# A graph network with a 64-expert layer: the experts' down products as three split matmuls

## What is computed

```python
hg = jnp.einsum('ecd,efd->ecf', expert_in, w_gate)      # 64 experts, up to 117 tokens each, 512 -> 256
hu = jnp.einsum('ecd,efd->ecf', expert_in, w_up)
expert_out = jnp.einsum('ecf,edf->ecd', jax.nn.silu(hg) * hu, w_down)   # 256 -> 512
```

## Time and profile before

| | us |
|---|---|
| median of three runs | 1040.75 (1038.95 to 1041.92) |
| the profiled execution, its own time | 1040.16 |
| its span | 1038.3 |
| product of the first expert to that of expert 62 (line 1375) | 684.05 to 1000.16 |
| one expert in that stretch | 5.10 |

### The profile page before, as it was taken

How to read it: one execution, slowest core, us unless ns; L and a number is a source line. 1 busy time by engine, 2 the same in 40 slices (tenths; PEclk the granted TensorE clock), 3 DMA queues, 4 the chain that set the end, 5 groups by cost and what they waited for, 6 DMA issues and landing times. The chain is left out here.

```text
span 1038.3 us, 13178 instructions
## 1 busy us (share of the span) xinstructions
PE 940.6 (91%) x4324; PEld 696.8 (67%) x4324; DVE 709.4 (68%) x1325; ACT 447.8 (43%) x694; POOL 392.2 (38%) x322
## 2 busy tenths in 40 slices
PE   2979598996999999998999989889999999999980
PEld 2879585443888778886788868666666666666650
DVE  4463548988665467678767786758777776766675
ACT  3442510013344353543444522466666666666640
POOL 4500000000750035410751115366666666666640
PEclk9985898998999999999999998989999999999995
DMA  6200003312420022201220052559999999999868
GB/s 173 83 1 1 1 1 118 121 57 88 133 72 23 1 80 92 83 1 51 87 86 17 20 186 87 187 196 328 338 339 334 355 333 324 380 348 345 312 161 209
DMA packets 57100, 159.73 MB, mean 154 GB/s; under 512 B 13840, under 2 KB 21590, under 8 KB 48595
## 3 DMA queue, kind: packets, MB, share of 16 engines
q1 hardware_dynamic: 44755, 147.63, 41.7%
q0 software_dynamic: 12288, 11.36, 3.8%
HBM read 152.71 MB, written 25.58 MB: 172 GB/s over the span
## 5 line engine op out<-in xcount | busy, mean ns | idle before, releaser
L260 PE MATMUL ps<-split_operands 128*125 128x512 f32 (+5 forms) x690 | 272.9, 396 | 31.4 <-DVE split_operands L986 5.7
L261 PE MATMUL ps<-split_operands 128*125 128x512 f32 (+5 forms) x690 | 266.1, 386 | 0.0
L262 PE MATMUL ps<-split_operands 128*125 128x512 f32 (+5 forms) x690 | 265.4, 385 | 0.0
L630 POOL DMA_INDIRECT yrow_scratch<-work,row_i x64 | 150.9, 2358 | 97.3 <-ACT work L891 94.8
L260 PEld LDWEIGHTS ps<-split_operands 128*125 128x125 f32 (+3 forms) x690 | 135.0, 196 | 61.3 <-issue 13.6
L376 POOL TENSOR_TENSOR split_operands<-work,split_operands 128x512 fp32r<-128x512 f32 x66 | 83.6, 1296 | 202.1 <-ACT split_operands L358 189.9
L262 PEld LDWEIGHTS ps<-split_operands 128*125 128x125 f32 (+3 forms) x690 | 135.2, 196 | 26.7
L261 PEld LDWEIGHTS ps<-split_operands 128*125 128x125 f32 (+3 forms) x690 | 135.6, 196 | 24.0
L1366 DVE TENSOR_TENSOR gate_up_lo<-expert_weights,split_operands 128x2048 fp32r<-128x2048 f32 x64 | 146.3, 2286 | 3.8 <-ACT split_operands L873 3.6
L873 ACT ACTIVATE split_operands<-expert_weights 128x2048 fp32r<-128x2048 f32 x64 | 121.9, 1905 | 3.2 <-DMA expert_weights<-experts_in 3.1
L1834 PE MATMUL ps<-expert_weights,work 128*117 128x512 f32 x256 | 120.3, 592 | 0.5 <-issue 0.5
(11 more groups left out here) (214 smaller groups left out, 1286.3 us busy)
## 6 DMA issues: line engine op xcount, KB each, us to landing
expert_weights<-experts_in SPq DMA_DIRECT2D x64, 1024.0 KB
expert_weights<-experts_in SPq DMA_DIRECT2D x64, 512.0 KB
work<-w_in SPq DMA_DIRECT2D x12, 1024.0 KB, 5.2
yrow_scratch<-work SPq DMA_DIRECT2D x5, 1500.0 KB
split_operands<-yrow_scratch SPq DMA_DIRECT2D x4, 1120.0 KB
work<-wmix_in SPq DMA_DIRECT2D x4, 1024.0 KB, 7.6
work<-cw_in SPq DMA_DIRECT2D x3, 1024.0 KB, 5.2
work<-rows_in SPq DMA_DIRECT2D x10, 256.0 KB, 4.7
```

What stands on the lines that cost most here:

```text
L260: pe.matmul(o, a[1], b[0], start=start, stop=False)
L261: pe.matmul(o, a[0], b[1], start=False, stop=False)
L262: return pe.matmul(o, a[0], b[0], start=False, stop=stop)
L630: pool.indirect_dma_start(yrow, bass.IndirectOffsetOnAxis(ap=row_i[:, e:e + 1], axis=0), OS[e % 4], None, bounds_check=last_row, oob_is_er ...
```

## The change

The down product of each expert is made as `gate_up` is, with `mm3`: both operands get a high and a low part.

- The down weights get a high part in one of two places (`DN_hi`), made by ACT in a new step `down_hi(e)`, and a low part in place in the ring (`DN_lo`), made by DVE in `down_lo(e)`.
- The copy at the end of `gated(e)` (line 1379) is gone. ACT makes the high part of the transposed hidden values out of PSUM (`h_part_hi(e)`), and DVE the low part (`h_part_lo(e)`), into a new tile `HTP`.
- `down(e)` issues six split matmuls in place of two fp32 ones and waits for `down_lo(e)` as well. `halves_done` counts the parts in their new order.
- Streams: ACT now runs `silu(e)`, `gate_up_hi(e+2)`, `scale(e-1)`, `h_part_hi(e)`, `down_hi(e+1)`, `xe_hi(e+2)`; DVE runs `gated(e)`, `gate_up_lo(e+2)`, `h_part_lo(e)`, `down_lo(e+1)`, `xe_lo(e+2)`, and `gates` where there is one.

```diff
+        DN_hi = [rg(o, 1024) for o in (16272, 32144)]
+        DN_lo = [sb(f"down_lo{r}", [P, 1024], F32R, at=rg_at + 4 * (o + WA)) for r, o in enumerate(ring_at)]
...
+        HTP = sb("hidden_pairs", [P, 8 * CAP], F32R, at=fg_at + 4 * 4416)
+        HTR = [(HTP[:, cut(4 * CAP * i, 2 * CAP)], HTP[:, cut(4 * CAP * i + 2 * CAP, 2 * CAP)]) for i in range(2)]
...
+        def halves_done(e, down):
+
+            if down:
+                return len(plan) + min(2 * e + 3, 2 * E)
+            return len(plan) + max(2 * e, 1)
...
+            def down_hi(e):
+                act.wait_ge(S(f"load_in{RINGS + e % RINGS}"), 16 * (e // RINGS) + 16)
+                if e >= 2:
+                    act.wait_ge(S("o_ps"), e - 1)
+                act.activation(DN_hi[e % 2], RING[e % RINGS][:, cut(WA, 1024)], ACT.Copy).then_inc(S("weight_hi"), 1)
+
+            def h_part_hi(e):
+                act.wait_ge(S("ht_ps"), NSH + e + 1)
+                if e >= 2:
+                    act.wait_ge(S("o_ps"), e - 1)
+                act.activation(HTR[e % 2][0][:, 0:2 * CAP], ps[:, 4 + e % 2, 0:2 * CAP], ACT.Copy).then_inc(S("ht_hi"), 1)
...
+            down_hi(0)
             for e in range(E):
                 silu(e)
                 if e + 2 < E:
                     gate_up_hi(e + 2)
                 if e >= 1:
                     scale(e - 1)
+                h_part_hi(e)
+                if e + 1 < E:
+                    down_hi(e + 1)
                 if e + 2 < E:
                     xe_hi(e + 2)
...
-                dve.wait_ge(S("weight_hi"), len(plan) + e + 1)
+                dve.wait_ge(S("weight_hi"), halves_done(e, False))
...
-                dve.wait_ge(S("ht_ps"), NSH + e + 1)
+
+            def down_lo(e):
+                dve.wait_ge(S("weight_hi"), halves_done(e, True))
+                dve.tensor_tensor(DN_lo[e % RINGS][:], RING[e % RINGS][:, cut(WA, 1024)], f(DN_hi[e % 2]), ALU.subtract).then_inc(S("weight_lo"), 1)
+
+            def h_part_lo(e):
+                dve.wait_ge(S("ht_hi"), NT * NL + e + 1)
                 if e >= 2:
                     dve.wait_ge(S("o_ps"), e - 1)
-                dve.tensor_copy(HTF[e % 2], ps[:, 4 + e % 2, 0:2 * CAP]).then_inc(S("ht_sb"), 1)
+                dve.tensor_tensor(HTR[e % 2][1][:, 0:2 * CAP], ps[:, 4 + e % 2, 0:2 * CAP], f(HTR[e % 2][0][:, 0:2 * CAP]),
+                                  ALU.subtract).then_inc(S("ht_sb"), 1)
...
+            down_lo(0)
             for e in range(E):
                 gated(e)
                 if e + 2 < E:
                     gate_up_lo(e + 2)
+                h_part_lo(e)
+                if e + 1 < E:
+                    down_lo(e + 1)
+                if e + 2 < E:
                     xe_lo(e + 2)
...
-                pe.wait_ge(S("weight_lo"), len(plan) + e + 1)
+                pe.wait_ge(S("weight_lo"), halves_done(e, False))
...
+                pe.wait_ge(S("weight_lo"), halves_done(e, True))
                 for k in range(2):
-                    last = pe.matmul(ps[0:CAP, 6 + e % 2, :], HTF[e % 2][:, cut(k * CAP, CAP)], RING[e % RINGS][:, cut(WA + 512 * k, 512)],
-                                     start=(k == 0), stop=(k == 1))
+                    last = mm3(ps[0:CAP, 6 + e % 2, :], sub(HTR[e % 2], A_, cut(k * CAP, CAP)),
+                               (DN_hi[e % 2][:, cut(512 * k, 512)], DN_lo[e % RINGS][:, cut(512 * k, 512)]), k == 0, k == 1)
```

## The result

The changed kernel takes 1057.13 us (median of four runs, 1054.55 to 1058.99), the kernel before beside it 1041.34 (1038.95 to 1043.64): a ratio of 1.0165, 95% interval 1.0128 to 1.0201. It is slower, by 1.3 to 2.0%. The forecast was 1056.5 us, slower with a chance of 0.91.

A forecast was written before the change was run, and what follows sets the result against it. PE was taken to bound the kernel before, a two-expert latency chain the changed one. 1040.16 + 11.5 (chain) + 4.4 (router's steps) = 1056.1, other terms 0; with the median above the profiled run, forecast 1056.5 us, range 1047 to 1069.

The forecast's parts named there:

- The main step: Loop from product(e-1) through PE, ACT and DVE to product(e+1) becomes the bound: 10.57 us for two experts, +11.5 us.
- One reading: In the kernel before, DVE's largest stall, after the product, waits until ACT has the high part of the next weights.
- PE's work: Six split matmuls of `down` take 1.40 us in place of 1.71: 0.31 less per expert, to 4.80.
- The router's steps: DVE steps between `xe_lo` and the next product, e = 2 to 9, now count in full: about +4.4 us.
- The clock: PE's clock stays at 1.00 through the stage.
- Transfers: Loads spread over 5.28 us per expert in place of 5.10, late ones rarer: taken as 0, up to +3 us allowed.
- POOL: `down_lo` may hold up scatters, with room for it; a scatter under way does not hold up `down_lo`: 0.
- rival 2: The same chain with a POOL scatter holding up `down_lo`: 18 us more, 1075; chance 0.07.
- Start and end: `down_hi(0)` and `down_lo(0)` fall into stalls before the first product; the last chain gains +0.4 - 0.3; both taken as 0.
- The first rival: PE stays the bound, 1021 us, or the transfers take over, 1030 to 1040; chance 0.06.

The follow-up runs named there:

- The filler in two places: ACT copy of 128 x 234 added to the changed kernel between `silu` and `gate_up_hi` (1064.7 us) or behind `down_hi` (1053.98); first place in kernel before: 1039.7.
- the transposes inside: Changed kernel with PE issuing the two transposes of product(e-1) after the first of four blocks of `gate_up(e)`, not ahead of it: 1039.9 us.
- a quarter of `down_lo`: Changed kernel with `down_lo` cut to 256 of 1024 columns, one matmul reading the high part instead of the low: 1037.89 us.
- both moves: Changed kernel with the transposes inside and the router's DVE steps moved to right behind the product: 1039.66 us, again 1036.68.
- the three orders: The last experiment: both moves, plus `transpose_x(e+2)` ahead of `down(e-1)` on PE and `xe_lo(e+2)` ahead of `down_lo(e+1)` on DVE: 1036.0 us.
- `down` inside too: Both moves, plus `down(e-2)` issued after the first block of `gate_up(e)`, ahead of the transposes: 1096.92 us.

## Why the prediction was right

**The main step held: a latency chain of two experts takes PE's place.** Forecast 10.57 us, measured 10.53, by steps 4.12 / 4.10, 0.28 / 0.28, 1.95 / 1.94, 2.20 / 2.21, 0.33 / 0.31, 1.14 / 1.13, 0.55 / 0.56. The mean of products 10 to 60 is 5.26 in place of 5.28, and it was 5.09: 5.264 - 5.092 over 62 experts is 10.7 us, forecast 11.5. The filler in two places and the transposes inside show that it is this chain. PE's period is 0.46 above its work of 4.80, as forecast (0.5), though only 0.33 of it counts as idle, since the modelled ends of its matmuls reach into the gaps; DVE is idle for 0.64 (forecast 0.75).

One reading was off and carried nothing. In the kernel before, DVE's largest stall is not the one for ACT's high part (3.6 us in all, seven times) but the one for PE's transposes, ahead of the copy: 61.8 us, before each of the 62. The two end almost together, though. In the earlier trace rows the high part is done at 869.27 and the copy starts at 869.00, so the copy did stand beside the wait for ACT, and its successor does not.

**PE's work.** Six matmuls follow each other by 0.23 us (868.30, 868.53 and so on to 869.46), so 1.40 in all as forecast, 0.31 less than before. It gave nothing, since PE waited; only in the last experiment does it show in full, for some twenty experts.

**The router's steps.** The first ten experts took 59.97 us for 51.32, 8.7 more. Of these 1.7 are the chain's and about 1.5 a drop of the clock, which leaves 5.4, forecast 4.4. The steps themselves take what they took:

```profile
705.20 0.48 DVE L1418 TENSOR_TENSOR work<-work 125x320 f32<-125x320 f32 x1
706.65 0.42 DVE L1401 TENSOR_TENSOR work<-ps,work 117x256 f32<-117x256 f32 x1
707.13 0.42 PE L1882 MATMUL ps<-ident,work 117*128 117x117 f32 x2 [1.83 <-DVE work L1401]
```

**The clock** was forecast to stay at 1.00, and did but for one place. PE had been idle for the 1.83 us above (in the window below it was busy for 3.17 of 5 us), and then:

```profile
700.00:705.00 5.00, 4.83 (x25) 3.53 (x23) 4.01 (x4) 4.54 (x7) 2.95 (x2) 1.00 0.82 252
705.00:710.00 5.00, 3.17 (x15) 2.31 (x14) 4.86 (x9) 2.99 (x5) 3.84 (x3) 0.83 0.95 300
710.00:715.00 5.00, 5.00 (x23) 3.94 (x22) 2.55 (x5) 2.67 (x4) 0.24 (x1) 0.82 0.78 263
```

The granted clock (third column from the right) fell from its 2.4 GHz to 1.2 GHz for some 3.5 us. From first matmul to `down` that `gate_up` took 4.41 us (707.72 to 712.13) in place of 2.88, so 1.5 us. The gap does not settle it, though. Both fillers in the changed kernel left PE idle for the same 1.83 and 1.82 us before the same transposes, and there the clock stayed at 1.00 and the product came 1.1 us sooner after the one before (5.05 for 6.15). So a drop here is one of two outcomes, and these runs do not show what decides.

**Transfers.** No `gate_up_hi` waited for a load; six had. The share of the stretch fell from 0.94 to 0.89. As forecast.

**POOL.** 62 `down_lo` took 1215 ns in the mean, no more than the one of the earlier trace rows, and nearly all began inside a scatter, so no scatter under way held them up: rival 2 is out. The other direction did show, and a little more than before: 59 scatters that started inside `gate_up_lo` took 2.41 us, and the gather, 1.08 before, took 1.19 when it started inside `down_lo`. POOL had room for it. The page "SBUF — State Buffer" of the Trainium skill (section "SBUF: two separate sides") says that whichever of the two starts first keeps the other out for its whole instruction, for a DVE instruction with two SBUF inputs only against a GpSimd one that reads SBUF. These traces agree only where DVE was first.

**Start and end, both put at 0, were off and cancel.** Product 0 came 4.58 us later, of which 4.1 were there before the experts began (the last product of the shared experts at 668.72 for 664.59); the clock was lower in this execution, 0.58 for 0.74 from 620 to 640 us. That is chance and not the change: over the twelve traces product 0 goes with the clock there (see the experiments), and with as much of the low clock as the kernel before had, changed kernels have it at 683.58 and 682.87, not later than its 684.05. The last product came 6.87 us after that of expert 62 for 6.31. And from the last product to the end of the span it was 28.0 us for 31.8. DVE waited less for the gathered rows of the first choices to be added after it, 0.35 us in the changed kernel

```profile
1034.58 3.40 DVE L1436 SCALAR_TENSOR_TENSOR x_out<-split_operands,work,x_out 125x512 f32<-125x512 f32 x5 [0.35 <-DMA split_operands<-yrow_scratch]
```

and 4.85 in the one before:

```profile
1016.03 3.40 DVE L1403 SCALAR_TENSOR_TENSOR x_out<-split_operands,work,x_out 125x512 f32<-125x512 f32 x5 [4.85 <-DMA split_operands<-yrow_scratch]
```

This repeats: with the filler in the changed kernel 27.2 and 27.8 us, in the kernel before 32.3, with a quarter of `down_lo` 31.5. So the slower loop gives 3 to 4 us back at its end. But the pace alone does not sort the runs: the router's steps moved early (5.27 per expert) had 29.2, the transposes inside (5.01) 29.1, both moves 29.8 and 29.5, the three orders (4.97) 28.9. I think that the rows' transfers find the loads done earlier; that is argued and was not tried, and the cause stays open. The sum is 4.58 + 17.57 + 0.56 - 3.81 = 18.9 us of span, where 15.9 were forecast. That the median came out within 0.6 us of the forecast is luck: several terms were off by 1 to 5 us and made up for each other. The stretch, +17.6 for +15.9, is the fair test.

**What I had not read**: the second chain at 5.0, just below; that DVE is full, at 5.58, in the experts with router steps; and how soon the loads come late below 5.0. None changes this forecast, but together they leave nothing to win: even with the orders put right, this change gives nothing. The first rival, faster by up to 19 us, was capped by the loads at 1030 to 1040, and the last experiment, with its other orders, landed there, at 1036.0.

## What to carry to other kernels

An engine that is 70% busy has no room to give if its idle time lies in front of one particular instruction: ask on which side of that stall the new work is placed, and add up the loop from this instruction through the other engines' streams back to it, over as many iterations as there are buffers. Work put behind the stall (here 1.47 us on DVE in each turn of two experts, for 0.31 us of PE saved in each expert) lengthens the loop; the same filler costs 7 to 8 us on the loop and nothing off it. Write down every such loop, not only the longest: a second at 5.0 us stood right under the first, and one move made a third of 6.06. And look at the next bound before spending effort on the first: the reorderings won back 1.8% (1.0165 to 0.9987 by the ratios) and ended at a full DVE in the first ten experts and at late loads in the second half.

## What was not expected of the hardware

In one execution PE fell to half its clock after an idle gap of 1.83 us in the middle of the busy stage, and stayed there for some 3.5 us. The run with the transposes inside did so too, after a gap of 1.83 us near product 1. But with either filler in the changed kernel the same gap at the same expert (1.83 and 1.82 us) was followed by no drop, nor were the gaps of 2.47 and 2.33 us near product 1 with both moves and with the three orders. With `down` inside too a gap of 1.06 us in every expert left the clock at 1.00 from 691 us to the end of the stage.

A `down_lo` of DVE that began inside a scatter of POOL took as long as any (1216 ns, 60 of them), while a scatter that began inside `gate_up_lo` took 2.41 us and ended 0.9 us after it, in the mean of 59.

Transfers that had a share of 0.94 in the kernel before were close behind PE: at 4.8 us per expert they held until product 35, with a share of 1.00 at 361 GB/s from 739 to 850 us, and then loads came late.
